# Layer 1 of the coupling net multiplied once per batch, its cycles combined on VectorE, steps in a staggered order

## The reference, cut to what matters

```python
gf = global_net(mean over tokens)              # one number per batch
for _ in range(3):                             # cycles
    h = gelu(out @ w1 + b1)                    # 256 -> 256   layer 1
    h = gelu(h @ w2 + b2)                      # 256 -> 128   layer 2
    h = gelu(h @ w3 + b3)                      # 128 -> 64    layer 3
    tf = sigmoid(h @ w4 + b4)                  # 64 -> 1      layer 4
    coupling = 0.1 + adaptive_range * (0.7 * gf + 0.3 * tf - 0.5) * 2.0
    out = out + coupling * twist(out)          # twist: [o_r,o_i,p_r,p_i] -> [p_r,-p_i,-o_r,o_i]
```

## Time and profile before

| | us |
|---|---|
| median of 3 runs (1358.65 to 1360.85) | 1358.72 |
| profiled execution, its own time | 1361.13 |
| its span, first to last instruction | 1359.1 |
| TensorE busy in it | 1133.3 (83%) |
| VectorE / ScalarE / GpSimd busy | 1149.4 / 737.0 / 871.9 |
| mean granted TensorE clock | 0.949 |

### The profile page before, as it was taken

One profiled execution on the slowest core, in us unless ns is written; L12 is line 12 of the kernel. 1 busy time (PEld: TensorE's weight loads), 2 busy tenths in 40 slices (PEclk: granted clock), 3 DMA queues, 4 the chain that ended last, 5 costly groups with the idle time before them and its releaser, 6 DMA issues. The chain is left out here.

```text
span 1359.1 us, 10889 instructions
## 1 busy us (share of the span) xinstructions
PE 1133.3 (83%) x2880; PEld 491.7 (36%) x2880; DVE 1149.4 (85%) x1628; ACT 737.0 (54%) x1267; POOL 871.9 (64%) x390
## 2 busy tenths in 40 slices
PE   3999985769778889878978987987896978799997
PEld 2344432223333334324324333433432423434443
DVE  4656676399999999999999999999999999746556
ACT  2554444757655756755656674665674433355442
POOL 0000000699989999998999999899999998000000
PEclk9999996798999999999999989999998988999998
DMA  6000000444535444354453544435435442000001
GB/s 201 0 1 1 0 0 1 140 135 146 180 102 185 132 149 155 124 185 134 146 179 113 174 146 139 151 124 186 154 127 184 155 156 78 0 0 0 32 31 62
DMA packets 46940, 146.47 MB, mean 108 GB/s; under 512 B 4448, under 2 KB 13280, under 8 KB 46880
## 3 DMA queue, kind: packets, MB, share of 16 engines
q1 hardware_dynamic: 46384, 144.96, 31.8%
q10 hardware_dynamic: 496, 0.82, 0.2%
HBM read 141.05 MB, written 4.72 MB: 107 GB/s over the span
## 5 line engine op out<-in xcount | busy, mean ns | idle before, releaser
L905 POOL TENSOR_TENSOR m_u<-m_dx,m_brow 128x1024 f32<-128x1024 f32 x256 | 596.7, 2355 | 1.0 <-DVE m_a_bank L988 0.9
L791 ACT ACTIVATE m_a_bank<-m_delta,m_negA 128x512 f32<-128x512 f32 x512 | 335.0, 683 | 171.6 <-DVE m_hc L1000 131.3
L1134 PE MATMUL m_y_bank<-m_hc,ident 128*128 128x512 f32 x640 | 333.1, 646 | 103.7 <-DVE m_hc L1000 103.7
L917 POOL TENSOR_TENSOR m_hc_pool<-m_hid,m_crow 128x1024 f32<-128x1024 f32 x96 | 226.0, 2354 | 28.5 <-DVE m_hid L988 28.1
L1134 PEld LDWEIGHTS m_y_bank<-m_hc,ident 128*128 128x128 f32 x640 | 120.1, 201 | 290.7 <-DVE m_hc L1000 170.5
L1000 DVE TENSOR_TENSOR m_hc<-m_a_bank,m_crow 128x512 f32<-128x512 f32 x320 | 202.5, 673 | 0.0
L926 POOL TENSOR_TENSOR m_dx<-m_delta,m_x 128x1024 f32<-128x1024 f32 x16 | 37.7, 2357 | 249.5 <-ACT m_delta L863 249.5
L988 DVE TENSOR_TENSOR_SCAN m_a_bank<-m_a_bank,m_carry,m_u 128x512 f32<-128x512 f32 x160 | 196.1, 1270 | 1.1 <-ACT m_a_bank L791 0.8
L988 DVE TENSOR_TENSOR_SCAN m_a_bank<-m_a_bank,m_u 128x512 f32<-128x512 f32 x160 | 186.6, 1212 | 7.1 <-POOL m_u L905 3.5
L1134 PE MATMUL m_y_bank<-m_hc_pool,ident 128*128 128x512 f32 x384 | 184.4, 603 | 5.6 <-POOL m_hc_pool L917 5.6
L333 PE MATMUL f_bank<-f_state,w 128*128 128x512 f32 x384 | 181.9, 603 | 0.0
(11 more groups left out here) (111 smaller groups left out, 1168.8 us busy)
## 6 DMA issues: line engine op xcount, KB each, us to landing
m_brow<-bc_rows SPq DMA_DIRECT2D x128, 512.0 KB, 4.8
m_crow<-bc_rows SPq DMA_DIRECT2D x128, 512.0 KB, 3.9
x_tok<-x_in SPq DMA_DIRECT2D x4, 1024.0 KB, 8.6
out<-x_tok SPq DMA_DIRECT2D x3, 1024.0 KB, 4.4
w<-w_in SPq DMA_DIRECT2D x1, 1024.0 KB, 11.4
out<-x_tok SPq DMA_DIRECT2D x2, 512.0 KB, 3.0
w<-w_in SPq DMA_DIRECT2D x1, 750.0 KB, 10.4
w<-w_in ACTq DMA_DIRECT2D x1, 512.0 KB, 5.9
```

What stands on the lines that cost most here:

```text
L791: nc.scalar.activation(a_bank[K % 2][:, j, :], delta[:, i % 2, c, :], ACT.Exp, scale=negA[:, c, n:n + 1]).then_inc(S["a"], 1)
L905: nc.gpsimd.tensor_tensor(u[:, K % U_RING, :, :], dx[:, i % 2, 2 * q:2 * q + 2, :], brow[:, K // 2 % ROW_RING, K % 2, :].unsqueeze(1).to_b ...
L917: nc.gpsimd.tensor_tensor(hc_pool[:, before % POOL_RING, :, :], hid[:, before % POOL_RING, :, :], crow[:, K // 2 % ROW_RING, K % 2, :].uns ...
L1134: op = nc.tensor.matmul(y_bank[:, j, :], ident[:, :], source[:, before % ring, j, :], start=False, stop=K % PASS == PASS - 1)
```

## The change

The state is no longer kept in channels. With J for the twist, a linear map with J(Jz) = -z, layer 1 of z + cJz is A + cB, where A = w1 z and B = w1 Jz. So:

- A and B are multiplied once per batch, from `z` (8 matmuls each; `neg_w` is a negated half of w1), and copied from PSUM to SBUF. Channels are given in the order [o_r, p_i, p_r, o_i] from the host, so that J swaps the two groups of 128 and changes one sign.
- Cycle 1 needs A + c0 B, cycle 2 (A + c0 B) + c1 (B - c0 A): `update()` does a product and a sum of 128x1024 per half, in cycles 0 and 1; `turn()` makes B - c0 A after cycle 0. Cycle 2 updates nothing.
- gelu of layer 1 reads SBUF. PSUM is four pairs of banks: 0 and 1 for side work in turn, 2 for layer 2, 3 for layers 3 and 4. ScalarE's copies and the transposes in take two banks at a time.
- The couplings of a batch are kept as rows of `stack` (two by a SyncE copy of 2 KB each from partition 0 of `cpl`, the third by the last tanh); "C" turns them to tokens (8 transposes of 34 rows), `coefficients()` makes the polynomial in c0, c1, c2 with operations of 128x8, and the end of a batch is x = x (1 + r) + shift + p z + q Jz in token order: for batches 0 and 1 `add_straight` and `add_across` on VectorE, for 2 and 3 ScalarE's `finish` and then `add_across`.
- Steps run in the order ORDER; in a step layers 3 and 4 of the step before come ahead of layer 2. The places of side work are a new list, BESIDE: step and place of the work, its kind, batch and number, step and place of its read. All four batches are normalised before the first update.
- Stores: one of 1024 KB per batch, on SyncE behind all row copies; before, the last batch went in two halves.

```diff
+    ORDER = [(0, 0), (1, 0), (0, 1), (1, 1), (0, 2), (2, 0), (1, 2), (3, 0), (2, 1), (3, 1), (2, 2), (3, 2)]
+    BESIDE = [
+        (HEAD, 0, "T", 0, 0, HEAD, 0), (HEAD, 0, "T", 0, 1, HEAD, 0),
+        (HEAD, 0, "A", 0, 0, HEAD, 0), (HEAD, 0, "A", 0, 1, 0, 1),
+        (0, 0, "B", 0, 0, 0, 2), (0, 1, "B", 0, 1, 0, 3), (0, 3, "g", 0, 0, 0, 4),
+        (0, 4, "T", 1, 0, 0, 5), (0, 4, "g", 0, 1, 0, 5), (0, 4, "T", 1, 1, 0, 5),
...
+        (6, 0, "C", 0, 0, None, None), (6, 0, "B", 3, 0, 6, 1), (6, 2, "g", 3, 0, 6, 3), (6, 4, "g", 3, 1, 7, 0),
+        (7, 0, "g", 3, 2, 7, 1), (7, 0, "B", 3, 1, 7, 1),
+        (8, 0, "C", 1, 0, None, None), (11, 4, "C", 2, 0, None, None), (TAIL, 1, "C", 3, 0, None, None),
...
# VectorE, update(s, h)
+                nc.vector.tensor_scalar(c, c, slope[:, 0:1], base[:, b:b + 1], ALU.mult, ALU.add).then_inc(coupling, 1)
+                nc.vector.tensor_tensor(to, b_[:, b % AB_RING, :, half(h)], over_m(c), ALU.mult).then_inc(scaled, 1)
+                nc.vector.tensor_tensor(to, to, other, ALU.add).then_inc(a_ready, 1)
# turn(s): part = a * c, b = b - part, each for two halves
# the order of VectorE's stream
+            for s in range(1, STEPS + 1):
+                ending = {6: 0, 8: 1}.get(s)
+                if ending is not None:
+                    coefficients(ending)
+                    add_straight(ending)
...
+                if cycle(s - 1) < CYCLES - 1:
+                    for h in range(HALVES):
+                        update(s - 1, h)
+                if ending is not None:
+                    add_across(ending)
+                if cycle(s - 1) == 0:
+                    turn(s - 1)
...
+                if s in (9, 10) and measure_next:
+                    measure(s - 9)
+            coefficients(2)
+            add_across(2)
+            coefficients(3)
+            if measure_next:
+                measure(2)
+            add_across(3)
# TensorE
+            for s in range(STEPS):
+                beside(s, 0)
                 if s > 0:
                     layer3(s - 1)
+                beside(s, 1)
                 if s > 0:
                     layer4(s - 1)
+                beside(s, 2)
                 layer2(s, 0)
+                beside(s, 3)
                 layer2(s, 1)
+                beside(s, 4)
# ScalarE
+                read(s, 0)
                 gelu1(s, 0, 0)
+                gelu1(s, 0, 1)
+                read(s, 1)
                 if s > 0:
                     gelu3(s - 1)
+                read(s, 2)
                 if s > 0:
                     tanh4(s - 1, 0)
                     tanh4(s - 1, 1)
                 gelu1(s, 1, 0)
                 gelu1(s, 1, 1)
                 read(s, 3)
                 gelu2(s, 0)
                 read(s, 4)
                 gelu2(s, 1)
+                read(s, 5)
...
+            finish(2)
+            finish(3)
```

More of the change, by code:

```diff
@@ L148, in done_count, with wait_kept, half, over_m @@
         def done_count(use):
-            return uses.index(use) + 1
+            return USES.index(use) + 1
         def wait_read(engine, use):
[L154 to L157, removed]
-            else:
-                engine.wait_ge(work_read, len(before) - backs)
-        def updates(s, h):
-            return (s * HALVES + h + 1) * 5
+            before = USES[:USES.index(use) + 1]
+            of_c = sum(u[0] == "C" for u in before)
+            if use[0] == "C":
+                engine.wait_ge(coef_read, of_c)
+            else:
+                engine.wait_ge(beside_read, len(before) - of_c)
+        def wait_kept(engine, s, h):
+            engine.wait_ge(kept[batch(s) % 2][h], 16 * (batch(s) // 2 * (CYCLES - 1) + cycle(s) + 1))
+        def half(h):
+            return slice(h * BANK, (h + 1) * BANK)
+        def over_m(t):
+            return t.unsqueeze(1).to_broadcast([P, KD, BANK])
+        def wait_added(engine, b):
+            engine.wait_ge(added, (b + 1) * BT * 2)
         @block.vector
@@ L238, in update @@
[L238 to L250, removed]
+                b, n = batch(s), coupled(s, h)
@@ L277, in _ @@
-            nc.vector.tensor_scalar(slope[:, :], w(w128, W128, "ar"), sign[:, 0:1], 0.3, ALU.mult, ALU.mult)\
-                .then_inc(constants, 1)
-            dve.wait_ge(constants, 1)
             moments_of((2, 3))
+            invert((2, 3))
+            normalise(2)
+            normalise(3)
             sum_up(1)
             coupling_base(0)
[L283 to L293, removed]
+            for s in range(1, STEPS + 1):
[3 more added lines that the diff above has]
+                    add_straight(ending)
+                if s == 2:
+                    coupling_base(1)
+                if cycle(s - 1) < CYCLES - 1:
@@ L396, in work @@
+                    if n == 1:
+                        last = nc.tensor.matmul(out[0:H3, 0, 0:1], w(w128, W128, "g2"), g1[:, b:b + 1],
                                                 start=True, stop=True)
                     else:
[L398 to L403 removed]
+                        last = nc.tensor.matmul(out[:, 0, 0:1], w(w64, W64, "g3"), g2[:, b:b + 1],
+                                                start=True, stop=True)
@@ L1207 @@
     build(nc, *args, out)
-    return run_bass_kernel_spmd(nc, [arrays], core_ids=[0]).results[0]["out"]
+    return run_bass_kernel_spmd(nc, [arrays], core_ids=[0]).results[0]["out"][..., order]
```

466 lines of the change are left out of this document (271 added, 195 removed), and 7 rows, old and new, of the table BESIDE.

## The result

| | before | after |
|---|---|---|
| median of 5 runs each, us | 1359.12 | 1351.26 (1350.04 to 1353.34) |
| profiled execution, us | 1361.1 | 1351.69 |
| its span, us | 1359.1 | 1349.9 |
| TensorE busy, us | 1133.3 | 1068.4 |

The ratio is 0.9942, 95% interval [0.9927, 0.9956]: 7.9 us less. That lies inside the range of the prediction (1343 to 1375), but the walk had said +0.2. In the profiled spans the first part ends 6.3 earlier (214.21 to 207.87), the scan stage takes 1.1 less (953.6 to 952.5, nothing in it was changed; from its table load to that of the second part it took between 950.8 and 953.5 in the traces of this study, so this 1.1 shows nothing), and the second part 1.8 less (191.3 to 189.5). TensorE's busy time fell by 64.9, as forecast; an eighth of it came through as time.

What follows compares the result with a forecast made beforehand. TensorE was taken to bound the kernel before, but not to stay the bound. The second part's +1.9 and the first part's -1.7 gave +0.2 on the profiled 1361.1; less 2.4 to the median, 1358.9 us, range 1343 to 1375.

Steps and rivals of the forecast that it cites:

- the walk: Both feed-forward parts followed through the engine queues: second part 1.9 us slower, first 1.7 faster, +0.2 in sum.
- a half batch of transposes in (16 records) 1.75: TensorE's price for transposing half a batch of z into channels: 16 records, 1.75 us.
- What TensorE gains: TensorE's work falls by 27.5 us in layer 1 and about 4 in transposes back: 31 per part, 62 in both.
- First part: First feed-forward part: same walk, A starting 20.65 us later, first transposes at low clock; 212.5 against 214.2, 1.7 faster.
- In the tail measure(2) hides behind finish(3): End of the first part: measure(2) costs no time, only measure(3) adds 3.4 us.
- the hole: Step 10's gelu1 waits 5.7 us for VectorE's late add; TensorE idles 6.6 and its clock falls.
- rival C: Small VectorE operations cost their upper bounds: +10.2 us in each part, 1379; chance 0.16.
- Rival A: VectorE catches up, so the hole and low clock go: 7.5 us in each part, 1344; chance 0.17.
- the ring: Steps 8 to 11: ScalarE and TensorE waiting on each other in turn set the step, about 8.2 us.
- Rival B: TensorE's sum decides, so waits vanish and late steps take 5.5: 52 us less, 1307; chance 0.07.
- Rival D: TensorE's clock stays at half in steps 9 to 11: +19 us, 1378; chance 0.10.
- the expected 31 us of a part: TensorE's forecast saving per part from fewer layer 1 matmuls and transposes back; the walk left 2.3 before the tail.

Runs made afterwards that it cites:

- Experiment 1: Changed kernel with each transpose of z into channels issued twice into the same place; 1362.82 us, ratio 1.0023 to the kernel before.
- experiment 3: Changed kernel with eleven more 128x512 matmuls per part inside A and B of batches 1 to 3 (steps 1 to 7); 1369.76 us, ratio 1.0073.
- experiment 4: Changed kernel with VectorE reordered: update(7), turn(7), update(8), update(9) ahead of batch 1's coefficients and additions, measure(0) and measure(1) moved; 1339.09 us, ratio 0.9849.
- experiment 2: Changed kernel with eleven more 128x512 matmuls per part in steps 8 to 11, result unread; 1352.81 us, ratio 0.9952.
- experiment 6: Changed kernel with batch 2's coefficients transposed ahead of layer 2 of step 11 and its straight term on VectorE, without finish(2); 1350.9 us, ratio 0.9935.
- experiment 8: Experiment 6 with two more 128x512 matmuls, result unused, behind layer 4 of step 10, during TensorE's wait; 1348.13 us, ratio 0.9914.
- experiment 10: Experiment 4 with coefficients(3) ahead of add_across(2) and the last store in two halves; 1337.89 us, ratio 0.9837.
- experiment 7: Experiment 6 with batch 2's coefficients transposed between the halves of layer 2 of step 11 instead of ahead of it; 1348.11 us, ratio 0.9913.

## Why the prediction was wrong

**The step that failed is a term in "Prices of what is new": "a half batch of transposes in (16 records) 1.75".** I had carried over from matmuls that an f32 operation leaves two records. A transpose leaves one: the 128 records of L441 in the page of after are 128 transposes (64 a part), and the 16 records in the earlier trace rows are the 16 transposes of a whole batch, not 8.

```profile
L441 PE MATMUL f_pair<-ident,f_z_tok 128*128 128x128 f32 x128 | 20.0, 311 | 31.1 <-DVE f_z_tok L223 27.2 <-ACT f_z L577 2.3 <-ACT f_b L584 1.6
```

A half batch is 8 records, 0.9 to 1.05. In each part T0 and T1 in the head and T2 and T3 in steps 1 and 4 stand in TensorE's queue, which sets the end there; the walk is late by 2.0, 3.7 and 5.4 just behind them in the second part, and by 5.1, 6.8 and 8.5 in the first. Experiment 1 gives the 1.75 back and lands at +11 against the change. The same slip hid itself in "What TensorE gains" ("32 transposes back (64 records)" were 64 transposes), where nothing hung on it, since the records' busy time was right.

The Trainium skill, TensorE: Matmul & The Clock Gate, "Terms", says that loads and matmuls of trn2 have a transpose mode, 4 times faster for FP32. The trace bears out that there is a difference: 128 columns at 0.43 for 512 twice would be 0.215, and a transpose took 0.11 to 0.13, so about half. What the page's four times are measured against, no run here shows.

**The same term at the start of the first part.** In "First part" A was to start at 28.6, behind transposes "at low clock, as the first ones before did". It started at 24.89 and ran at 0.43 a record. Timeline of the first part, timeline of the second, and a window of the first:

```profile
21.60 3.45 PE L441 MATMUL f_pair<-ident,f_z_tok 128*128 128x128 f32 x16 [21.60 <-DVE f_z_tok L223]
24.89 1.02 PE L453 MATMUL f_pair<-f_z,w 128*128 128x512 f32 x2
```

```profile
1163.70 3.67 PE L441 MATMUL f_pair<-ident,f_z_tok 128*128 128x128 f32 x16 [5.59 <-DVE f_z_tok L223]
```

```profile
20.00:25.00 5.00, 3.40 (x17) 3.43 (x18) 4.93 (x19) 1.02 (x1) 0.00 (x0) 1.00 0.89 335
```

The forecast gave the first 16 transposes 6.9 (21.7 to 28.6), for 32 records; they took 3.3 up to A, 0.21 each. This is nearly all of the 3.7. The 0.21 is the pace of the second part's first 16 (3.5 up to A, at a granted clock of 0.50 from 1164 to 1167), so the forecast's low clock fits the pace, though the window says 1.00. The window of before says 1.00 too, and there the first two of the four records in the earlier trace rows started 0.86 apart, twice 0.43. Which of the two, pace or granted clock, is right in the first microseconds of the program stays open.

**An error of opposite sign.** "In the tail measure(2) hides behind finish(3)" was wrong by 2.6: the additions follow finish(3) tile by tile with 0.74 of wait, so measure(2)'s 3.35 stood in their way. The first part's tail took 19.1, not 16.15.

**What is given back** from tanh(7) on, 5.45 to 3.7 in the second part: a 128x128 addition starts every 0.26 (walk 0.2, upper bound 0.35), eight straight ones take 3.26 (2.8), so the hole is 6.33 and not 5.7; the step behind it takes 9.57, not 9.0; the tail 17.95, not 17.5. About 0.6 of it is the clock's; the rest, 1.2, is an eighth of rival C's 10.2. The 9.57 is no fixed price: behind the same hole that step took 9.27 in the first part, 8.52 in experiment 1 and 8.32 in experiment 3. In the first part 4.0 is given back, 2.9 of it in the tail.

**The sum and luck.** With half batches of 8 records the walk would have said some 14 less in both parts together (5.45 and 8.6, as late as it was at tanh(7)); the span fell by 9.2, and what was given back is the rest. That the measured time lies inside the range is luck: the range was set by rivals A and C, and neither happened.

**What held.** Head, seven steps bound by TensorE and four by the ring (8.3 to 8.4 a step, forecast 8.2), one hole at step 10, one fall of the clock in that hole in each part (and one at each part's end, where TensorE has no more work), a tail of three dependent passes (timeline of VectorE in the tail; DMA issue of the row copies):

```profile
1338.00 0.23 DVE L285 COPY f_coef<-f_pair 128x8 f32<-128x8 f32 x2
...
1340.76 0.35 DVE L327 SCALAR_TENSOR_TENSOR x_tok<-f_z_tok,f_coef,x_tok 128x128 f32<-128x128 f32 x1 [0.74 <-ACT x_tok L562]
```

```profile
f_stack<-f_cpl SPq DMA_DIRECT2D x32, 2.0 KB, 1.6
```

The wide operations cost what the slope gave (128x1024 starts every 1.14 to 1.26, record 1.23), the row copies were hidden, the store took 4.5 (4.4). Rival A did not happen, but its price for the hole, 7.5 a part, is what experiment 4 measured in the second part (7.45); with a step behind the hole between 8.32 and 9.57, the agreement to a tenth is luck. Rival B is excluded by experiments 2 and 3 together. Rival D did not happen in this kernel; experiments 6 and 8 show that one more wait of 1.38 brought a fall in one of its steps.

**Where the expected 31 us of a part went.** In the second part, beside the trace of before: the head costs 11.7 more (38.4 against 26.7, it took on A and B of batch 0 and the transposes of batch 1), steps 1 to 7 take 91.3 against 100.3 (tanh(7) of before is at 1294.87), steps 8 to 11 take 41.9 against 51.0, and the tail 17.9 against 13.2: 1.7 less. The relief falls into the late steps, which take the ring's 8.3 at the least in this kernel, and lost 7.5 to VectorE's hole; the early ones hold all products that are left and stay bound by TensorE.

## What to carry to other kernels

Before a count of records is turned into a count of instructions, check it for each form by itself against the source: one wrong factor of two, in a queue that bounds the stage, was more than the whole of this miss. When work is taken from the bounding engine, ask in which steps it is taken: put the same small extra in each regime (experiments 2 and 3) and the kernel tells what a microsecond is worth there. When a unit of work ends in the middle of a sequence, put its long last pass behind the updates on which the next steps wait: on top of the change that move was worth more than the change itself (12.6 against 7.9).

## What the runs showed of the hardware that was not expected

An f32 transpose of 128x128 leaves one record and takes 0.11 to 0.13, an f32 matmul two (0.43 each for 512 columns). A single wait of 1.38 of a TensorE that had run at full clock through gaps of 0.79 was followed by a granted clock of 0.50, which cost the step 2.8; two useless matmuls in the wait gave it back. A wait of 1.38 is not always followed by a fall: the last coefficients' transposes wait 1.38 in the changed kernel too, and their 8 took 0.65 there, 1.03 in experiment 10.

```profile
1333.30 0.65 PE L461 MATMUL f_pair<-ident,f_stack 34*128 34x34 f32 x8 [1.38 <-issue]
```

Shorter waits were followed by one as well. In the second part of experiments 6, 7 and 8 the clock fell ahead of tanh(8), in experiment 7 from 1296.5 to 1297 (0.84, then 0.50), behind waits of 0.66, 0.78 and 1.15; the changed kernel had 0.65, 0.78 and 0.84 there and kept 1.00. tanh(8) came 1.0 later for it, and the hole behind took 0.7 of that back. That the 1.15 brought it down is not tested. Timeline of TensorE, experiment 7 and after:

```profile
1296.54 1.82 PE L429 MATMUL f_pair<-f_h,w 64*128 64x512 f32 x4 [1.15 <-ACT f_h L536]
```

```profile
1297.26 1.13 PE L428 MATMUL f_pair<-f_h,w 64*128 64x512 f32 x4 [0.84 <-ACT f_h L535]
```
